# A graph network on one core: layer one reads a count matrix for near targets only, and gathers the rows of the far ones

## The reference

```python
def _L0_gnn_ref(x, edge_index, W1, b1, W2, b2, W3, b3):
    row, col = (edge_index[0], edge_index[1])
    n = x.shape[0]
    deg = jnp.clip(jax.ops.segment_sum(jnp.ones_like(row, dtype=x.dtype), row, num_segments=n), 1.0)
    def mp(h):
        agg = jax.ops.segment_sum(h[col], row, num_segments=n)
        return jax.nn.relu(agg / deg[:, None])
    h = mp(x @ W1.T + b1)
    h = mp(h @ W2.T + b2)
    return h @ W3.T + b3
```

## Time and profile before

| | |
|---|---|
| median of three timed runs | 5644.15 us (5638.18 to 5647.6) |
| span of the profiled execution | 5632.1 us |
| median less span | 12.05 us; the profiled execution has no time of its own beside its span |
| PE busy, granted TensorE clock | 81%, mean 0.912 |
| DVE, ACT, POOL busy | 52%, 26%, 41% |
| build, from 75 us to the first read of the matrix | 842 us |
| first pass, second pass of layer one | 436 us, 447 us |
| all behind them | 3832 us |

### The profile page before, as it was taken

The page is one execution under the profiler, slowest core; times in us unless marked ns, Lnnn a source line. Parts: engine busy times, 40 slices in busy tenths (PEclk is TensorE's granted clock), DMA queues, the critical chain, the costliest instruction groups (busy, mean ns, idle before and its releaser), DMA issues. The chain is left out here.

```text
span 5632.1 us, 79313 instructions
## 1 busy us (share of the span) xinstructions
PE 4580.5 (81%) x27606; PEld 3050.1 (54%) x27606; DVE 2934.3 (52%) x7168; ACT 1480.3 (26%) x2691; POOL 2325.5 (41%) x2401
## 2 busy tenths in 40 slices
PE   4677665998997877778886999799979967777776
PEld 3443333444443555655443666466656556777765
DVE  6788976885113867663555221512152254444554
ACT  1466473001002865521112010201020032222222
POOL 0000000000001777606551676267527737777774
PEclk7798886998998999978998999899989989999998
DMA  5365877998996243418457887888788655555553
GB/s 163 70 111 128 143 144 171 204 206 179 211 210 153 75 121 107 125 55 267 159 163 252 261 271 230 277 258 267 215 296 266 203 155 145 144 146 151 147 152 84
DMA packets 1573721, 998.04 MB, mean 177 GB/s; under 512 B 691836, under 2 KB 1502375, under 8 KB 1573239
## 3 DMA queue, kind: packets, MB, share of 16 engines
q1 hardware_dynamic: 1232314, 635.72, 44.3%
q0 software_dynamic: 87024, 200.23, 12.3%
q10 hardware_dynamic: 253965, 156.72, 9.2%
HBM read 666.89 MB, written 160.08 MB: 147 GB/s over the span
## 5 line engine op out<-in xcount | busy, mean ns | idle before, releaser
L1192 PE MATMUL ps<-adj_d,xs_d 128*128 128x512 bf16 (+3 forms) x8526 | 1810.7, 372 | 139.1 <-DVE xs_d L1143 139.1
L1192 PEld LDWEIGHTS ps<-adj_d,xs_d 128*128 128x128 bf16 x8526 | 846.3, 102 | 1012.4 <-DVE xs_d L1143 144.7
L2671 POOL DMA_INDIRECT rows_mg<-p_tab,src_idx x784 | 756.5, 965 | 274.9 <-issue 238.6
L1096 POOL DMA_INDIRECT rows_d<-xh_tab,src_idx x632 | 616.3, 975 | 503.2 <-POOLq L174 215.6
L814 PE MATMUL ps<-hot,lo 128*128 128x500 bf16 (+7 forms) x1800 | 491.4, 393 | 264.3 <-DVE hot L745 117.3
L1096 POOL DMA_INDIRECT rows_d<-x_tab,src_idx x512 | 496.1, 969 | 480.2 <-POOLq L174 256.6
L860 ACT CAST slab<-ps 128x500 f32 (+6 forms) x530 | 458.0, 864 | 373.1 <-PE ps L832 247.8
L1721 POOL DMA_INDIRECT rows_g<-x_tab,src_idx x444 | 434.1, 978 | 164.1 <-issue 128.5
L2768 PE MATMUL ps<-win_mg,turned_hot_mg 128*128 128x128 f32 x1568 | 340.1, 302 | 195.8 <-DVE pre_mg L2720 195.7
L1175 PEld LDWEIGHTS ps<-onehot_d,rows_d 128*128 128x128 f32 x3552 | 430.6, 193 | 61.3 <-DVE onehot_d L1114 33.4
L1175 PE MATMUL ps<-onehot_d,rows_d 128*128 128x72 f32 (+1 forms) x3552 | 423.6, 276 | 26.3 <-DVE onehot_d L1114 26.3
(11 more groups left out here) (365 smaller groups left out, 6550.5 us busy)
## 6 DMA issues: line engine op xcount, KB each, us to landing
adj_d<-adjacency SPq DMA_DIRECT2D x140, 812.0 KB
adj_d<-adjacency SPq DMA_DIRECT2D x84, 857.5 KB
attr_mg<-in_edge_attr SPq DMA_DIRECT2D x195, 256.0 KB
xp_g<-x_tab SPq DMA_DIRECT2D x70, 448.0 KB
k_rows_d<-k_tab ACTq DMA_DIRECT2D x56, 448.0 KB
loc_mg<-loc_rows SPq DMA_DIRECT2D x196, 128.0 KB
adjacency<-slab SPq DMA_DIRECT2D x4, 4900.0 KB
q_s<-q_tab SPq DMA_DIRECT2D x42, 448.0 KB
```

Source lines behind the costliest of these rows:

```text
L1096: nc.gpsimd.indirect_dma_start(rows[:, q % GR * K + k, :], None, table, bass.IndirectOffsetOnAxis(ap=src_idx[:, j:j + 1], axis=0)).then_in ...
L1192: last = nc.tensor.matmul(ps[:, m % 2, 0:w], xs[:, g * GW + k, e, :], adj[:, slot, k, 0:w], start=(g == 0 and k == 0 and e == 0), stop=(g ...
L2671: nc.gpsimd.indirect_dma_start(rows[:, q % RR, k, :], None, p_tab, bass.IndirectOffsetOnAxis(ap=src_idx[:, j:j + 1], axis=0)).then_inc(row ...
```

## The change

The matrix now holds only the first 576 tiles of edges, in 324 units; its reader in layer one uses only the 26 blocks of targets below 3328 (`NEARBY`, `BOUND`). Its chunks are of 12 units in the middle and at most 304 columns wide, 20 of them as before.

The edges with a target from 3328 on lie in the last 220 tiles (`FT`). The build sorts them by source block on the chip: POOL makes a one-hot of the source block for each of these tiles (`far_hot`), PE sums the blocks before it and the edges before it within a tile (`sum_prior`, `sum_rank`), DVE picks each edge's rank in its block (`pick`), and from block and rank follows a slot, of which each source block has 640 (five columns of 128, `CAP`). POOL writes each edge's code to its slot in DRAM with 220 indirect DMAs of 128 elements of 4 B, over 16 tables; SP reads the tables back, DVE adds them and unpacks index and low source bits. The counts that the matrix gave before are made beside it: for sources 208 small products (`count_sources`), for targets 220 (`count_targets`), the latter from one-hots that POOL makes after its scatters.

In each pass of layer one (`source_pass`) a strip has 4 groups of 7, 7, 6 and 6 blocks. POOL gathers, for each of 49 source blocks, five times 128 rows, and PE adds them into the strip's sums with five float32 matmuls against a one-hot that DVE makes. One such block stands behind each group from the fourth on.

```diff
-           Class(504, 644, 1, 20, 25),
-           Class(644, USED, 1, 25, 20))
+           Class(504, 576, 1, 20, 25))
+UT = CLASSES[-1].end
 Unit = namedtuple("Unit", "tile tiles width per_bank banks")
 UNITS = [Unit(t, c.tiles, c.width, c.per_bank, -(-WIN // c.per_bank)) for c in CLASSES for t in range(c.begin, c.end, c.tiles)]
-CHAIN, EVEN, STEP = 49, 98, 24
-COLUMNS = (128, 352, 256, 304, 352, 400, 448, 496, 400, 304, 320, 336, 336, 368, 368, 368, 400, 400, 416, 448)
-FIRSTS = (0, CHAIN) + tuple(range(EVEN, len(UNITS), STEP))
+CHAIN = 49
+Even = namedtuple("Even", "first step count")
+EVENS = (Even(74, 12, 15), Even(254, 24, 3))
+COLUMNS = (128, 152, 200) + (144, 152, 160, 176, 192, 200, 208, 224, 232, 240, 248, 256, 272, 272) + (304, 304, 304)
+FIRSTS = (0, CHAIN) + tuple(e.first + n * e.step for e in EVENS for n in range(e.count))
...
+NEARBY = 26
+BOUND = NEARBY * P
+FAR = 564
+FT = TILES - FAR
+CAP = 5
+SLOTS = WIN * CAP
+ROOM = P * SLOTS
+PLANES = 16
+PARTS = (7, 7, 6, 6)
+BEGINS = (0, 7, 14, 20)
+RANKED = 10
+RANKS = FT // RANKED
+COUNTED = TILES - UT
...
+                        pool.wait_ge(batched, 1)
+                        for c in range(RANKS):
+                            for n in range(c * RANKED, (c + 1) * RANKED):
+                                last = nc.gpsimd.tensor_scalar(far_hot[:, n, :], iota_bf[:, 0:WIN], far_hi[:, n:n + 1], None, ALU.is_equal)
+                            last.then_inc(far_made, 1)
+                        pool.wait_ge(prior_kept, 1)
+                        for c in range(RANKS):
+                            if c >= 2:
+                                pool.wait_ge(rank_summed, c - 1)
+                            nc.gpsimd.tensor_tensor(spread[c % 2][0:WIN, :, :], ident[0:WIN, 0:WIN].unsqueeze(1).to_broadcast([WIN, RANKED, WIN]),
+                                                    prior[0:WIN, c * RANKED:(c + 1) * RANKED].unsqueeze(2).to_broadcast([WIN, RANKED, WIN]),
+                                                    ALU.mult).then_inc(spread_made, 1)
+                        pool.wait_ge(blanked, 16 * PLANES)
+                        pool.wait_ge(placed, 1)
+                        for n in range(FT):
+                            k = n % PLANES
+                            if n >= PLANES:
+                                pool.wait_ge(sent[k], 16 * (n // PLANES))
+                            nc.gpsimd.indirect_dma_start(slot_tabs[k], bass.IndirectOffsetOnAxis(ap=slot_at[:, n:n + 1], axis=0),
+                                                         far_code[:, n:n + 1], None).then_inc(sent[k], 16)
+                        for n in range(FT):
+                            if n >= ENDS:
+                                pool.wait_ge(dst_counted, n - ENDS + 1)
+                            nc.gpsimd.tensor_scalar(end_lo[:, n % ENDS, :], iota_bf[:, :], far_dlo[:, n:n + 1], None, ALU.is_equal).then_inc(ends_made, 1)
+                            nc.gpsimd.tensor_scalar(end_hi[:, n % ENDS, :], iota_bf[:, 0:WIN - NEARBY], far_dhi[:, n:n + 1], None,
+                                                    ALU.is_equal).then_inc(ends_made, 1)
...
+                        def keep_prior():
+                            dve.wait_ge(prior_summed, 1)
+                            nc.vector.tensor_copy(prior[0:WIN, :], ps[0:WIN, 7, 0:FT]).then_inc(prior_kept, 1)
+                        def pick(c):
+                            dve.wait_ge(rank_summed, c + 1)
+                            if c:
+                                dve.wait_ge(ranked, c)
+                            nc.vector.tensor_tensor(picked[:, :, :], ps[:, 7, 0:RANKED * WIN].rearrange("p (t h) -> p t h", h=WIN),
+                                                    far_hot[:, c * RANKED:(c + 1) * RANKED, :], ALU.mult).then_inc(picked_made, 1)
+                            dve.wait_ge(picked_made, c + 1)
+                            nc.vector.tensor_reduce(rank[:, c * RANKED:(c + 1) * RANKED], picked[:, :, :], AX.X, ALU.add).then_inc(ranked, 1)
+                        def far_lo_hot(n):
+                            if n >= LOS:
+                                dve.wait_ge(src_counted, n - LOS + 1)
+                            nc.vector.tensor_scalar(far_lo1[:, n % LOS, :], iota16[:, :], far_lo[:, UT - FAR + n:UT - FAR + n + 1], None,
+                                                    ALU.is_equal).then_inc(lo_made, 1)
...
+                        dve.wait_ge(slots_in, 16 * PLANES)
+                        dve.wait_ge(unpacked, 12)
+                        nc.vector.tensor_reduce(slot_sum[:, :], slots[:, :, :].rearrange("p w j -> p j w"), AX.X, ALU.add).then_inc(unpacked, 1)
...
+                        dve.wait_ge(dst_counted, FT)
+                        nc.vector.tensor_copy(far_deg[:, :], ps[:, 7, 0:WIN - NEARBY]).then_inc(ends_kept, 1)
...
+                        def sum_prior(c):
+                            pe.wait_ge(shaped, 5)
+                            pe.wait_ge(far_made, c + 1)
+                            for t in range(c * RANKED, (c + 1) * RANKED):
+                                last = nc.tensor.matmul(ps[0:WIN, 7, 0:FT], far_hot[:, t, :], later[:, FT - 1 - t:2 * FT - 1 - t],
+                                                        start=(t == 0), stop=(t == FT - 1))
...
+                        def sum_rank(c):
+                            pe.wait_ge(spread_made, c + 1)
+                            if c:
+                                pe.wait_ge(picked_made, c)
+                            nc.tensor.matmul(ps[:, 7, 0:RANKED * WIN], before[:, :], far_hot[:, c * RANKED:(c + 1) * RANKED, :].rearrange("p t h -> p (t h)"),
+                                             start=True, stop=False)
+                            nc.tensor.matmul(ps[:, 7, 0:RANKED * WIN], ones_mat[0:WIN, :], spread[c % 2][0:WIN, :, :].rearrange("p t h -> p (t h)"),
+                                             start=False, stop=True).then_inc(rank_summed, 1)
+                        def count_sources(n):
+                            pe.wait_ge(lo_made, n + 1)
+                            nc.tensor.matmul(ps[:, 6, 0:WIN], far_lo1[:, n % LOS, :], far_hot[:, UT - FAR + n, :], start=False, stop=False).then_inc(src_counted, 1)
+                        def count_targets(n):
+                            pe.wait_ge(ends_made, 2 * n + 2)
+                            if n == 0:
+                                pe.wait_ge(picked_made, RANKS)
+                            nc.tensor.matmul(ps[:, 7, 0:WIN - NEARBY], end_lo[:, n % ENDS, :], end_hi[:, n % ENDS, :],
...
+                            if c == end - 1:
+                                for k in range(PLANES):
+                                    sp.wait_ge(sent[k], 16 * len(range(k, FT, PLANES)))
+                                for k, tab in enumerate(slot_tabs):
+                                    sp.dma_start(slots[:, k, :], tab[0:ROOM, :].rearrange("(p j) w -> p (j w)", p=P)).then_inc(slots_in, 16)
...
+                            sp.dma_start_transpose(adj[:, t % RING, 0:PARTS[g], 0:w],
+                                                   adjacency[c:c + w, BEGINS[g] * P:(BEGINS[g] + PARTS[g]) * P]).then_inc(adj_in[t % RING], 16)
+                    @block.gpsimd
+                    def _(pool):
+                        for v in range(WIN):
+                            if v >= RW:
+                                pool.wait_ge(window_done, v - RW + 1)
+                            for k in range(CAP):
+                                j = window_of(v) * CAP + k
+                                nc.gpsimd.indirect_dma_start(rows[:, v % RW, k, :], None, table,
+                                                             bass.IndirectOffsetOnAxis(ap=slot_idx[:, j:j + 1], axis=0)).then_inc(rows_in[v % RW], 16)
...
+                        for t in range(tiles):
+                            m, g, c, w = place(t)
+                            beside(nc.tensor, t)
+                            if m == 0:
+                                pe.wait_ge(low, g + 1)
+                            if g == 0 and m >= 2:
+                                pe.wait_ge(stored, m - 1)
+                            pe.wait_ge(adj_in[t % RING], 16 * (t // RING + 1))
+                            for k in range(PARTS[g]):
+                                for e in range(TERMS):
+                                    last = nc.tensor.matmul(ps[:, m % 2, 0:w], xs[:, BEGINS[g] + k, e, :], adj[:, t % RING, k, 0:w],
+                                                            start=(g == 0 and k == 0 and e == 0), stop=False)
+                            last.then_inc(used, 1)
+                            v = window_at(t)
+                            if v is not None:
+                                pe.wait_ge(matched, v + 1)
+                                pe.wait_ge(rows_in[v % RW], 16 * CAP * (v // RW + 1))
+                                to = g * P if m else 0
+                                for k in range(CAP):
```

(29 more changed lines are left out.)

408 lines of the change are left out of this document (310 added, 98 removed).

## The result

5476.3 us (median of four runs, 5472.7 to 5484.7) against 5641.2: a ratio of 0.971, interval 0.9695 to 0.9726. The forecast was 5267 us. The change saves 165 us where 377 were forecast; the forecast's range (5185 to 5350) misses it. That holds on the chip of this comparison and on chips like it.

What follows compares the result with a forecast made beforehand. TensorE and the DMA engines were taken as full in the passes before, POOL's gathers as the limit after. Build -155, passes -225.1 and `prepare` +3 gave -377: span 5255, time 5267 us, range 5185 to 5350.

Steps and rivals of the forecast that it cites:

- C: Rival, chance 0.04: every indirect DMA at pitch 2.13 us; passes +196 us, first pass at 881, total 5807 us.
- The pairs' price: Build's end: 220 pairs of POOL's target one-hots at 0.42 us each, PE's matmuls waiting for them, 92 us.
- (a): Build, units 16 to 48: chain of 220 matmuls of 220 columns on PE; between 0 and 48 us, 15 taken.
- (c): Build, units 100 to 250: 208 one-hots on DVE and 208 matmuls on PE; between 0 and 59 us, 25 taken.
- (b): Build, units 53 to 97: 22 rounds alternating PE, DVE and POOL; between 10 and 48 us, 20 taken.
- The chain of writes: Build: each chunk's write issued when the one before has landed; write 3 at 285, write 16 at 630.
- The writes' price: Build: each narrow chunk write 24 us, handover included, or 27 us while the scatters run.
- rival A: Chance 0.22: narrow writes cost by their bytes and units set the pace; first pass at 696, total 5201 us.
- Rival B: Chance 0.17: writes and scatters hinder each other, 37 us a write while scatters run; first pass at 834, total 5339 us.
- The passes: Layer one's two passes: POOL's 245 gathers, 311.2 us, set each; 325.5 and 332.0 us against 435.7 and 446.9, together -225.1.
- third limit: Passes: the DMA engines' matrix read plus 20 gathers, 23.1 us a strip, against POOL's 25.4.
- last write and handover: End of the build: the last chunk's write and its handover take 26 us, against 29.3 before.

## Why the prediction was wrong

The sign was right, and so was the mechanism at the build's end (PE waits for L812 and L813) and in the first pass; the build was mis-sized. The first read came at 962, 197 us later than the forecast's (762, and 3 for `prepare`), and that is nearly all of the miss. No rival had it so late; C had 881.

**The pairs' price** was the step that failed: 0.294 for the one-hot of 128 columns and 0.127 for the other, 0.42 a pair, 92 us in all. From the first product (708) to the last (923) it took 215, 123 more. The row beside it was of another instruction: an affine select without an operand per partition, 294 ns; a comparison with one takes 600 at the same size, 340 at 23 columns, and 630 and 426 on average, with DVE at work. The last paragraph of the prediction did name a pair at 0.8 us as a sign of being wrong, but its spread and its range had no upper end for the pair, as (a) to (c) had. The Trainium skill ("GPSIMD Engine Reference", 3.1 Elementwise) measures a factor of 1.96 between POOL and DVE, for an add of two float32 tensors of 2048 elements. The two versions here, 1.06 against 0.53 us a pair, have 2.0 for a short comparison, another form. From DVE's own row, 285 ns for 128 columns, twice the time would have been 0.57 for the larger one-hot, an estimate: 61 of the 123 us. The smaller one has no such row.

**(a) and (b)** came to 32 us more at write 3 (317 instead of 285). (a) cost 19 us instead of 15 (write 0 at 197.5, before at 178.3). (b) cost 48 instead of 20, the top of its bounds. In it the float32 product took 1.7 us (two records of 0.863), not 1, at a granted clock of 0.72, and DVE waited 24 us for it; with `pick` one tile later unit 97 was in 18 us sooner. PE's, DVE's and POOL's busy times were counted; their waits for one another were not.

**The chain of writes**: 381 us from write 3 to write 16 instead of 345. Write 3, which the first scatters meet, took 36.3 instead of 27. Writes 4 to 14 came 28.5 apart instead of 27, and the last two took 32.2 and 27.3 instead of 24 each. The scatters took 1.55 us each, not 1.27, but nothing waited for that.

**The writes' price**, 24 us, was right for a wrong reason, which is luck. The 256 B chunk was quick because it starts at column 0, not for its size, so rival A rested on a row that didn't show what I read into it. The rule of the Trainium skill that I weighed ("DMA: Bandwidth & Descriptors", Specifications: below 512 B a descriptor is read, changed and written back) isn't what decides here either: aligned writes of 256 to 448 B took 7 to 12 us, and misaligned ones of 576 B 25 or more. Rival B's price would have been the nearest to the result (5339), by a mechanism of which the trace shows little (writes beside scatters came 28.5 us apart, not 37).

**The passes**: 329.3 us instead of 325.5, and 352.7 instead of 332.0. POOL's gathers took 310 us in both, as said (311.2). The first pass was bound as said, with PE close behind: without a fifth of the gathers, some 61 us of POOL's, it fell by 19. The second ended 41 us behind its last gather, where the forecast had 21; PE had waited 29.4 us for the matrix. The forecast had put this third limit, the DMA engines, 2.3 us a strip below POOL's and given it no wait.

**What the others gave**: last write and handover 34 instead of 26, the layers behind +7. The median of after lies 8 us below its profiled run, whose time is 1.8 us above its span; I had added 12 us. These two took 19 us off the miss, by luck.

Rival C, the slower side, got 0.04, with gathers at 2.1 us. On the second kind the sign did turn, but a gather took 0.96 + 0.30 us there too. Their mean distance was 1.45 us because POOL had waits, some for PE and most called "remote" in the trace, with no engine named; what lies behind them is open.

## What to carry to other kernels

Price an operation on another engine from a row of the same form (same operand kinds), or from the engine that does it now times a factor, and keep the upper end until a trace has it. Where work is given to the idle engine, ask who will wait for it: 220 pairs in 58 units made POOL the limit, in 212 units on DVE they cost nothing that the total shows. And look at the address of a write before its size.

## What the runs showed of the hardware

- Rows written from SBUF to DRAM at an address 2 B below a multiple of 64 B: 22 to 31 us for 6272 rows of 256 to 576 B; on multiples of 64 B 7 to 13 us. Multiples below 64 B weren't tried.
- POOL's comparison with an operand per partition: 0.34 us for 23 columns, 0.60 for 128 (bf16); DVE's, at work beside others: 0.25 and 0.28.
- Small scatters (128 of 4 B, one in 1.55 us) put the chunks' writes 28.5 us apart instead of 25.7. On the second kind of chip, with up to 16 of them under way and no chunk being written, ACT and DVE act on PE's products 22 to 25 us late; with at most four, issued more slowly and almost always beside a chunk's write, no unit stood still.
- A kernel full of indirect DMAs differs by 10% between chips (5640 and 6215 us), and the order of two kernels can turn with it: compare on the same chip, and on more than one.
